# A running maximum over 512 positions, taken as four chunks of 128 on four partitions and spread by transposes

## The chip, the cores and the metric

The kernel runs on one core of a Trainium2 chip. The metric is the device time of one execution in microseconds (us): the median of several runs. The core has five engines that run side by side and wait for one another by semaphores: PE (TensorE, matrix products), DVE (VectorE), ACT (ScalarE), POOL (GpSimd) and SP (SyncE, here a queue of transfers).

## The reference

`x` is 8 rows of 512 positions of 128 numbers. Each row goes through a layer norm with a per-row scale and shift, then through a gated recurrent attention (head size 64), is added to `x`, and then goes through a second norm and a mixture of 8 experts of which each position takes 2. All of it is in 32-bit floating point. The part that the change touches is the running maximum `m_t` of the recurrence:

```
m_t = maximum(zf_t + m, zi_t)
i_p = exp(zi_t - m_t)
f_p = exp(zf_t + m - m_t)
C_t = f_p * C + i_p * (v_t k_t^T)
n_t = f_p * n + i_p * k_t
h   = o_t * (C_t q_t) / max(|n_t . q_t|, 1)
```

With F_t the running sum of `zf` and a_t = zi_t - F_t, the maximum less F_t is M_t = max(a_1 ... a_t). The whole recurrence of a row is then a masked product: the weight of position s in position t is exp(a_s - M_t) for s <= t.

## The kernel before

Every engine has its own program, written out by hand. A program is a sequence of bodies, one for each value of `b` from -2 to 7, and each body walks 16 steps `t` from 3 to 18. In one body three rows are in hand at once. Row `b` passes through the experts. Row `b+1` finishes its attention and computes its expert gates (the parts called `end`). Row `b+2` starts its attention (the parts called `start`, present for b = -2 to 5, eight bodies). In bodies 0 to 5 all three are there; these are called the full turns here. In bodies -2 and -1 there is no expert work yet, so POOL has nothing to split, and PE fills its time with products that `keep_busy` issues.

The expert work sets the pace. It has N = 16 pieces n (8 experts of 2 halves). For each, PE makes an "up" product in three parts (L1000 to L1002) into one of four banks; DVE clips and gates it into `hg` (L797); ACT rounds it into `hg_hi` (L498); the remainder `hg_lo = hg - hg_hi` is made by POOL (L446) for pieces 1 and 8 to 15 and by DVE (L809) for the others; and three steps later PE makes the "down" product in three parts (L1009, L1010, L1020). Each engine puts the attention's and the gates' operations between these pieces, in the order of the program text. Below, hg(12) means the `hg` of piece 12, and up(13) the up product of piece 13.

The stretch around the change is steps 11 to 15 of the row that starts:

- DVE makes `a_col` (L769): 128 partitions, 4 columns, one column for each chunk of 128 positions.
- PE turns it into one row of 512 on one partition by four transposes (L941), then makes the scores of chunk 0 (L877, L878).
- DVE runs a scan with max over that row (L773, `m_row`). The scan stands behind hg(12), the difference `top_d` of the two best expert logits (L684) and the four index searches (L686), and ahead of hg(13).
- PE spreads `m_row` over 128 partitions by a product of depth one with a row of ones (L952), into bank `bB`.
- DVE adds the causal mask (`mb`, L776); ACT makes the weights `ew` = exp(a_s - M_t) from it (L477, L479).

The gates of the other row are made in the same steps on DVE: `top_d`, the index searches, then, behind hg(13), `top_s`, `gate_a`, `gate_b`, `top_g` (L731, L734), two products and the sum `gates` (L739), and after that `mb`. On ACT the exponential `top_e` of `top_d` (L529) stands in step 12, between `hg_hi` of piece 11 and of piece 12, since an engine takes its instructions in order:

```
if live(t - 1):
    act.wait_ge(s_hg, b * N + t)
    a.activation(hg_hi[k][:, :], hg[k][:, :], ACT.Copy)
if t == 12 and end:
    act.wait_ge(s_td, m1 + 1)
    a.activation(top_e2[:, :], top_d[:, :], ACT.Exp)
```

In step 14 PE transposes the gates into bank 3 (L1027). ACT then makes the first `ew` (which waits for `mb`) and after it copies the gates out (`gate_rows` L541, `gateT` L542). Bank 3 is also the bank of every fourth up product, so up(15) waits for `gateT`.

Of the kernel before, what the change touches and what calls it, by code (L numbers as in the profile page):

```python
# [5 lines left out]
def adaln_mlstm_moe_kernel(  # L6
# [42 lines left out]
    ALU = mybir.AluOpType  # L49
    ACT = mybir.ActivationFunctionType  # L50

    P = 128
    B, T, D = x_in.shape
# [3 lines left out]
    NT = T // P  # L57
# [8 lines left out]
    NVO = NZ + DH  # L66
# [15 lines left out]
    with ctx:  # L82
        def sb(name, shape, dt=fp32):
            return ctx.enter_context(nc.sbuf_tensor(name, shape, dt))

        def sem(name):
            return ctx.enter_context(nc.semaphore(name))


        ident = sb("ident", [P, P])  # L90
# [3 lines left out]
        mean_col = sb("mean_col", [P, 1])  # L94
        neg_row = sb("neg_row", [1, T])
        iota_e = sb("iota_e", [P, E])
# [64 lines left out]
        a_col = sb("a_col", [P, NT])  # L161
        m_row = sb("m_row", [1, T])
        mb = sb("mb", [P, NT, P])
# [88 lines left out]
        s_a = sem("s_a")  # L252
        s_aT = sem("s_aT")
        s_M = sem("s_M")
        s_Mb = sem("s_Mb")
# [130 lines left out]
        def _(pool):  # L386
# [13 lines left out]
            g.memset(mean_col[:, :], 1.0 / D).then_inc(s_const, 1)  # L400
            g.memset(neg_row[:, :], -3e38).then_inc(s_const, 1)
            for e in range(E):
# [152 lines left out]
        def _(dve):  # L555
# [12 lines left out]


            v.memset(gateT[:, :].bitcast(fp32), 0.0).then_inc(s_zero, 1)  # L570

# [92 lines left out]
            def body(b, end, start, ahead, live, first=False):  # L664
                m1, m2 = b + 1, b + 2

                def middle(t):

                    if end:
# [6 lines left out]
                        if t == 11:  # L676

                            dve.wait_ge(s_lgp, m1 + 1)
                            v.tensor_tensor(lg[:, :, :], bC[:, 0:NT * E].rearrange("p (j e) -> p j e", j=NT),
                                            br_bc[:, :].unsqueeze(1).to_broadcast([P, NT, E]), ALU.add).then_inc(s_lg, 1)  # L680
                        if t == 12:

                            dve.wait_ge(s_mx, m1 + 1)
                            v.tensor_tensor(top_d[:, :], mx[:, :, 1], mx[:, :, 0], ALU.subtract).then_inc(s_td, 1)  # L684
                            for j in range(NT):
                                last = v.max_index(ix[:, j, :], mx[:, j, :], lg[:, j, :])  # L686
                            last.then_inc(s_ix, 1)
# [24 lines left out]
                def after(t):  # L712
# [27 lines left out]
                    if start:  # L740
# [29 lines left out]
                        if t == 12:  # L770

                            dve.wait_ge(s_aT, m2 + 1)
                            v.tensor_tensor_scan(m_row[0:1, :], bA[0:1, :], neg_row[0:1, :], -3e38, ALU.max, ALU.max).then_inc(s_M, 1)  # L773
                        if t == 13:
# [61 lines left out]

            F0 = 8
            pv = bA[:, 0:NT * NS].rearrange("p (j n) -> p j n", j=NT)
# [12 lines left out]
        def _(pe):  # L851
# [28 lines left out]
            def chain(b, end, start, t):  # L880
# [47 lines left out]
                if start:  # L928
# [9 lines left out]
                    if t == 12:  # L938
                        pe.wait_ge(s_a, m2 + 1)
                        for j in range(NT):  # L940
                            last = t_.transpose(bA[0:1, j * P:(j + 1) * P], a_col[:, j:j + 1], ident[:, :])  # L941
                        last.then_inc(s_aT, 1)
                        if end:

                            pe.wait_ge(s_lg, m1 + 1)
                        pe.wait_ge(s_qz, m2 + 1)
                        scores(0, bC[:, 0:T])
                    if t == 13:

                        pe.wait_ge(s_zo, m2 + 1)  # L950
                        pe.wait_ge(s_M, m2 + 1)
                        t_.matmul(bB[:, :], ones[0:1, :], m_row[0:1, :], start=True, stop=True).then_inc(s_Mb, 1)  # L952
                    if t == 14:
# [105 lines left out]

            F0 = 8  # L1060
            body(-2, False, True, True, lambda n: False, first=True)
# [32 lines left out]
```

## Time and profile before

| What | Value |
|---|---|
| time, median of 3 runs | 358.75 us (358.61 to 359.09) |
| time of the profiled execution | 354.73 us |
| its span, first to last instruction | 353.0 us |
| busy: PE, DVE, ACT, POOL | 320.5, 279.6, 158.6, 170.1 us |
| chain that ended last, by engine | PE 43%, DVE 37%, POOL 5%, DMA 4%, ACT 4% |
| mean granted clock of PE | 0.984 of full speed |

The busy time of an engine is the time in which it has an instruction in hand; matrix products overlap, so a busy PE need not be at its peak. The chain is the sequence of work that ended last, followed back from the last instruction, at each step to what released it or to the instruction before it on its engine. A timeline row gives the start of an instruction, its duration, engine, line, operation, output and inputs with their shapes, and in brackets the engine's idle time before it and what ended that.

### The profile page before, as it was taken

What the parts mean: (1) busy time and instruction counts of PE and PEld (TensorE: products, weight loads), DVE (VectorE), ACT (ScalarE), POOL (GpSimd) and SP (SyncE); (2) the same over time, 40 slices, a digit from 0 to 9 for tenths busy, and PEclk for the clock granted to TensorE, in tenths of its full rate; (3) what the DMA queues carried; (4) which work ended last, traced back from release to release, by engine and by line L of the source; (5) the groups of instructions that cost most, each with busy time, mean ns of one, the idle gap of its engine ahead of it and who ended that gap; (6) DMA issues with size and microseconds to landing.
All of it is one profiled execution on the core that took longest, in us unless ns stands there. A gap on an engine that the chain in (4) does not pass through costs nothing.

```text
span 353.0 us, 4976 instructions
## 1 busy us (share of the span) xinstructions
PE 320.5 (91%) x1712; PEld 257.9 (73%) x1712; DVE 279.6 (79%) x799; ACT 158.6 (45%) x292; POOL 170.1 (48%) x177
## 2 busy tenths in 40 slices
PE   2999978799899998999899989998999989887995
PEld 2887865678587867887687858785888668665883
DVE  5576783699869996899699987999679967775774
ACT  1432423254454636545546554544545354244442
POOL 7610640158544772387417852485406821583340
PEclk9999996899999999999999999999999999999999
DMA  4850001500061005200160007000610053004301
GB/s 127 266 155 0 2 0 42 200 2 0 2 238 32 3 0 183 88 0 1 63 208 2 0 8 254 10 0 0 229 45 0 0 154 117 1 1 124 147 0 30
DMA packets 13710, 24.13 MB, mean 68 GB/s; under 512 B 1771, under 2 KB 8086, under 8 KB 12662
## 3 DMA queue, kind: packets, MB, share of 16 engines
q1 hardware_dynamic: 13458, 23.69, 20.7%
q8 instruction: 13, 0.21, 0.2%
q14 instruction: 11, 0.09, 0.1%
q10 hardware_dynamic: 164, 0.07, 0.1%
q0 software_dynamic: 64, 0.07, 0.1%
HBM read 21.59 MB, written 2.23 MB: 67 GB/s over the span
## 4 chain that ended last, share of the span: by engine, by line
PE 43%; DVE 37%; POOL 5%; DMA 4%; ACT 4%; issue 4%; SPq 1%; DVEq 0%; POOLq 0%
DVE hg L797 10%; PE bank L1000 5%; PE bank L1002 5%; PE bank L967 5%; PE bank L1001 5%; PE bank L1010 4%; PE bank L1009 4%; PE bank L1020 4%; DVE hg_lo L809 2%; PE bank L900 2%; DVE stats L560 2%; DVE m_row L773 2%; DMA gate_bc<-gates_d 2%; DVE zp L759 2%; DVE zo L748 2%
## 5 line engine op out<-in xcount | busy, mean ns | idle before, releaser
L446 POOL TENSOR_TENSOR hg_lo<-hg,hg_hi 128x512 fp32r<-128x512 f32 x69 | 88.1, 1286 | 81.2 <-ACT hg_hi L498 81.2
L797 DVE SCALAR_TENSOR_TENSOR hg<-bank,neg_b,gate_bc 128x512 f32<-128x512 f32 x128 | 94.6, 743 | 35.9 <-PE bank L1002 24.0
L498 ACT ACTIVATE hg_hi<-hg 128x512 fp32r<-128x512 f32 x128 | 79.7, 628 | 90.6 <-DVE hg L797 89.2
L1000 PE MATMUL bank<-h_hi,w_hi 128*128 128x512 f32 x128 | 58.4, 456 | 9.7 <-ACT gateT L542 9.7
L1010 PE MATMUL bank<-hg_hi,w_lo 128*128 128x512 f32 x128 | 51.1, 399 | 0.0
L1001 PE MATMUL bank<-h_hi,w_lo 128*128 128x512 f32 x128 | 50.9, 397 | 0.0
L1002 PE MATMUL bank<-h_lo,w_hi 128*128 128x512 f32 x128 | 50.8, 397 | 0.0
L1009 PE MATMUL bank<-hg_hi,w_hi 128*128 128x512 f32 x128 | 50.6, 395 | 0.0
L1020 PE MATMUL bank<-hg_lo,w_hi 128*128 128x512 f32 x128 | 50.5, 394 | 0.0
L415 POOL TENSOR_SCALAR var_eps<-mv 128x4 f32<-128x4 f32 x16 | 4.9, 305 | 80.4 <-DVE mv L566 80.4
L809 DVE TENSOR_TENSOR hg_lo<-hg,hg_hi 128x512 fp32r<-128x512 f32 x59 | 42.3, 718 | 0.5
L1000 PEld LDWEIGHTS bank<-h_hi,w_hi 128*128 128x128 f32 x128 | 24.4, 191 | 20.2 <-issue 10.7
L1002 PEld LDWEIGHTS bank<-h_lo,w_hi 128*128 128x128 f32 x128 | 24.3, 190 | 5.8
L1010 PEld LDWEIGHTS bank<-hg_hi,w_lo 128*128 128x128 f32 x128 | 24.2, 189 | 5.8
L1009 PEld LDWEIGHTS bank<-hg_hi,w_hi 128*128 128x128 f32 x128 | 24.2, 189 | 5.7
L1020 PEld LDWEIGHTS bank<-hg_lo,w_hi 128*128 128x128 f32 x128 | 24.2, 189 | 5.6
L1001 PEld LDWEIGHTS bank<-h_hi,w_lo 128*128 128x128 f32 x128 | 24.5, 191 | 4.0 <-issue 1.4
L477 ACT ACTIVATE ew<-mb,a_col 128x128 f32<-128x128 f32 x32 | 11.7, 391 | 24.9 <-DVE mb L776 24.9
L967 PEld LDWEIGHTS bank<-vs,ew 128*128 128x128 f32 x160 | 19.4, 196 | 4.1 <-DVE ew L662 3.7
L967 PE MATMUL bank<-vs,ew 128*128 128x65 f32 x160 | 19.5, 278 | 3.1 <-DVE ew L662 3.1
L974 PEld LDWEIGHTS bank<-ones,ident 128*128 128x128 f32 x108 | 16.1, 216 | 5.3 <-issue 5.1
L422 POOL TENSOR_TENSOR rstd<-var_eps,minus_half 128x4 f32<-128x4 f32 x16 | 19.3, 1204 | 0.0
(163 smaller groups left out, 552.4 us busy)
## 6 DMA issues: line engine op xcount, KB each, us to landing
gate_bc<-gates_d SPq DMA_DIRECT2D x8, 1024.0 KB, 7.1
gate_bc<-gates_d SPq DMA_DIRECT2D x16, 256.0 KB, 3.7
gate_bc<-gates_d SPq DMA_DIRECT2D x8, 512.0 KB, 4.9
out_dram<-x_all SPq DMA_DIRECT2D x8, 256.0 KB, 2.3
w_raw<-in_L_ffn_W_dram SPq DMA_DIRECT2D x1, 1024.0 KB, 8.6
x_all<-in_L_attn_x_dram SPq DMA_DIRECT2D x2, 256.0 KB, 3.8
wmod_sb<-in_L_wmod_dram SPq DMA_DIRECT2D x1, 384.0 KB, 4.4
gates_d<-gate_rows SPq DMA_DIRECT2D x8, 16.0 KB
```

The source lines that it names most:

```text
L422: g.tensor_tensor(rstd[k][:, :], var_eps[k][:, :], minus_half[:, :], ALU.pow).then_inc(s_rs[k], 1)
L446: g.tensor_tensor(hg_lo[k][:, :], hg[k][:, :], hg_hi[k][:, :].bitcast(fp32), ALU.subtract).then_inc(s_lo_pool, 1)
L498: a.activation(hg_hi[k][:, :], hg[k][:, :], ACT.Copy).then_inc(s_hghi, 1)
L797: v.scalar_tensor_tensor(hg[k][:, :], up_bank[n % 4][:, :], neg_b1[:, n:n + 1], gate_bc[own % 2][:, n // NU, :], ALU.max, ALU.mult).then_i ...
L809: v.tensor_tensor(hg_lo[k][:, :], hg[k][:, :], hg_hi[k][:, :].bitcast(fp32), ALU.subtract).then_inc(s_lo_dve, 1)
L967: last = t_.matmul(bA[:, q * NS:(q + 1) * NS], ew[:, o:o + P], vs[:, j, :], start=j == 0, stop=j == q)
L1000: t_.matmul(dst, w_hi, hx, start=True, stop=False)
L1001: t_.matmul(dst, w_lo, hx, start=False, stop=False)
L1002: t_.matmul(dst, w_hi, hl, start=False, stop=True).then_inc(s_up, 1)
L1009: t_.matmul(y_bank[:, :], w_hi, hg_hi[k][:, :], start=n == 0, stop=False)
L1010: t_.matmul(y_bank[:, :], w_lo, hg_hi[k][:, :], start=False, stop=False)
L1020: t_.matmul(y_bank[:, :], w_hi, hg_lo[k][:, :], start=False, stop=n == N - 1).then_inc(s_dn, 1)
```

## The change

The transposed `a_col` is left as four rows of 128 on four partitions (one transpose in place of four), at a free place in bank `bA`. DVE scans the four chunks side by side (`m_chunk`). PE transposes the result back into columns, twice: each position's own value, and each chunk's last value repeated over all partitions. A second scan of three elements makes the maximum over the chunks before (`m_before`, whose first column is set to -3e38 once), and one operation takes the larger of the two (`m_col`). PE then spreads each column of `m_col` by a transpose of a broadcast 128x128 operand, four in all, in place of the product of depth one. The scan of the chunks moves ahead of `top_d` on DVE; PE waits for it behind the scores of chunk 0.

```diff
-        neg_row = sb("neg_row", [1, T])
+        neg = sb("neg", [P, P])
...
-        m_row = sb("m_row", [1, T])
+        m_chunk = sb("m_chunk", [NT, P])
+        m_before = sb("m_before", [P, NT])
+        m_col = sb("m_col", [P, NT])
...
-            g.memset(neg_row[:, :], -3e38).then_inc(s_const, 1)
+            g.memset(neg[:, :], -3e38).then_inc(s_const, 1)
...
+            v.memset(m_before[:, 0:1], -3e38).then_inc(s_Mz, 1)
...
+                    if t == 12 and start:
+
+                        dve.wait_ge(s_aT, m2 + 1)
+                        v.tensor_tensor_scan(m_chunk[:, :], bA[0:NT, M0:M0 + P], neg[0:NT, :], -3e38, ALU.max, ALU.max).then_inc(s_Mc, 1)
+                    if end:
                         if t == 12:
 
                             dve.wait_ge(s_mx, m1 + 1)
...
-                            dve.wait_ge(s_aT, m2 + 1)
-                            v.tensor_tensor_scan(m_row[0:1, :], bA[0:1, :], neg_row[0:1, :], -3e38, ALU.max, ALU.max).then_inc(s_M, 1)
+                            dve.wait_ge(s_McT, m2 + 1)
+                            v.tensor_tensor_scan(m_before[:, 1:NT], bA[:, M1 + NT:M1 + 2 * NT - 1], neg[:, 0:NT - 1], -3e38,
+                                                 ALU.max, ALU.max).then_inc(s_Mp, 1)
+                            dve.wait_ge(s_Mp, m2 + 1)
+                            v.tensor_tensor(m_col[:, :], bA[:, M1:M1 + NT], m_before[:, :], ALU.max).then_inc(s_M, 1)
...
-                        for j in range(NT):
-                            last = t_.transpose(bA[0:1, j * P:(j + 1) * P], a_col[:, j:j + 1], ident[:, :])
-                        last.then_inc(s_aT, 1)
+                        t_.transpose(bA[0:NT, M0:M0 + P], a_col[:, :], ident[:, :]).then_inc(s_aT, 1)
                         if end:
 
                             pe.wait_ge(s_lg, m1 + 1)
                         pe.wait_ge(s_qz, m2 + 1)
                         scores(0, bC[:, 0:T])
+
+                        pe.wait_ge(s_Mc, m2 + 1)
+                        t_.transpose(bA[:, M1:M1 + NT], m_chunk[:, :], ident[0:NT, 0:NT])
+                        t_.transpose(bA[:, M1 + NT:M1 + 2 * NT], m_chunk[:, P - 1:P].to_broadcast([NT, P]),
+                                     ident[0:NT, 0:NT]).then_inc(s_McT, 1)
...
-                        t_.matmul(bB[:, :], ones[0:1, :], m_row[0:1, :], start=True, stop=True).then_inc(s_Mb, 1)
+                        for j in range(NT):
+                            last = t_.transpose(bB[:, j * P:(j + 1) * P], m_col[:, j:j + 1].to_broadcast([P, P]), ident[:, :])
+                        last.then_inc(s_Mb, 1)
...
-            F0 = 8
+            F0, M0 = 8, 2 * NVO + 8
+            M1 = M0 + P
```

On DVE, step 12 of a full turn, from hg(12) to `top_s`. Before (a scan is listed under the name SCALAR_TENSOR_TENSOR; the brackets name the semaphores that an instruction waits for):

```order
L797 SCALAR_TENSOR_TENSOR hg<-bank,neg_b,gate_bc 128x512 [waits s_up]
L684 TENSOR_TENSOR top_d<-mx 128x4 [waits s_mx]
L686 MAX_INDEX ix<-mx,lg 128x8 x4
L773 SCALAR_TENSOR_TENSOR m_row<-bank,neg_row 1x512 [waits s_aT]
L797 SCALAR_TENSOR_TENSOR hg<-bank,neg_b,gate_bc 128x512 [waits s_up]
L691 TENSOR_SCALAR top_s<-top_e 128x4 [waits s_te]
```

The same place after the change:

```order
L812 SCALAR_TENSOR_TENSOR hg<-bank,neg_b,gate_bc 128x512 [waits s_up]
L691 SCALAR_TENSOR_TENSOR m_chunk<-bank,neg 4x128 [waits s_aT]
L696 TENSOR_TENSOR top_d<-mx 128x4 [waits s_mx]
L698 MAX_INDEX ix<-mx,lg 128x8 x4
L785 SCALAR_TENSOR_TENSOR m_before<-bank,neg 128x3 [waits s_McT]
L788 TENSOR_TENSOR m_col<-bank,m_before 128x4 [waits s_Mp]
L812 SCALAR_TENSOR_TENSOR hg<-bank,neg_b,gate_bc 128x512 [waits s_up]
L703 TENSOR_SCALAR top_s<-top_e 128x4 [waits s_te]
```

The scan that stood behind `top_d` and the index searches stands ahead of them, shorter, and two small operations take its old place ahead of hg(13).

On PE, steps 12 and 13 of a full turn, from the transposes of `a_col` to the spread of the maximum. Before:

```order
L941 MATMUL bank<-ident,a_col 1x128 [waits s_a]
L941 MATMUL bank<-ident,a_col 1x128 x3
L877 MATMUL bank<-qq,kk 128x512 [waits s_qz,s_lg]
L878 MATMUL bank<-qz,kk 128x512
L1000 MATMUL bank<-h_hi,w_hi 128x512 [waits s_hg]
L1001 MATMUL bank<-h_hi,w_lo 128x512
L1002 MATMUL bank<-h_lo,w_hi 128x512
L1009 MATMUL bank<-hg_hi,w_hi 128x512 [waits s_hghi]
L1010 MATMUL bank<-hg_hi,w_lo 128x512
L1020 MATMUL bank<-hg_lo,w_hi 128x512 [waits s_lo_pool]
L952 MATMUL bank<-m_row,ones 128x512 [waits s_M,s_zo]
```

The same place after the change:

```order
L956 MATMUL bank<-ident,a_col 4x128 [waits s_a]
L893 MATMUL bank<-qq,kk 128x512 [waits s_qz,s_lg]
L894 MATMUL bank<-qz,kk 128x512
L964 MATMUL bank<-ident,m_chunk 128x4 [waits s_Mc]
L965 MATMUL bank<-ident,m_chunk 128x4
L1021 MATMUL bank<-h_hi,w_hi 128x512 [waits s_hg]
L1022 MATMUL bank<-h_hi,w_lo 128x512
L1023 MATMUL bank<-h_lo,w_hi 128x512
L1030 MATMUL bank<-hg_hi,w_hi 128x512 [waits s_hghi]
L1031 MATMUL bank<-hg_hi,w_lo 128x512
L1041 MATMUL bank<-hg_lo,w_hi 128x512 [waits s_lo_pool]
L972 MATMUL bank<-ident,m_col 128x128 [waits s_M,s_zo]
```

Three transposes go; two small ones, with a wait for the scan, now stand between the scores and up(13); and four transposes stand where the product of depth one stood.

## Rows read from the trace of the kernel before

**Rows 1.** The page, the chain that ended last, by engine.
```profile
PE 43%; DVE 37%; POOL 5%; DMA 4%; ACT 4%; issue 4%; SPq 1%; DVEq 0%; POOLq 0%
```
**Rows 2.** The chain in order of time (start, us, what): row 0, then a full turn.
```profile
27.70 1.06 PE bank L952 x2
...
209.02 0.49 ACT gateT L542
...
222.44 0.44 PE bank L910 x4
```
**Rows 3.** Timeline of DVE in the same full turn, steps 12 and 13 (start, us).
```profile
201.72 0.75 DVE L797 SCALAR_TENSOR_TENSOR hg<-bank,neg_b,gate_bc 128x512 f32<-128x512 f32 x1
202.38 0.26 DVE L684 TENSOR_TENSOR top_d<-mx 128x4 f32<-128x4 f32 x1
...
203.12 1.19 DVE L773 TENSOR_TENSOR_SCAN m_row<-bank,neg_row 1x512 f32<-1x512 f32 x1
204.25 0.71 DVE L797 SCALAR_TENSOR_TENSOR hg<-bank,neg_b,gate_bc 128x512 f32<-128x512 f32 x1
204.89 0.24 DVE L691 TENSOR_SCALAR top_s<-top_e 128x4 f32<-128x4 f32 x1
...
205.44 0.16 DVE L734 TENSOR_TENSOR top_g<-top_g,top_e 128x4 f32<-128x4 f32 x1
...
205.87 1.17 DVE L739 TENSOR_TENSOR gates<-gate_a,gate_b 128x32 f32<-128x32 f32 x1
206.97 0.68 DVE L776 TENSOR_TENSOR mb<-bank,far 128x512 f32<-128x512 f32 x1
```
**Rows 4.** Timeline of POOL in the same stretch.
```profile
201.33 1.29 POOL L446 TENSOR_TENSOR hg_lo<-hg,hg_hi 128x512 fp32r<-128x512 f32 x1 [0.59 <-ACT hg_hi L498]
202.57 1.29 POOL L446 TENSOR_TENSOR hg_lo<-hg,hg_hi 128x512 fp32r<-128x512 f32 x1
203.82 1.28 POOL L446 TENSOR_TENSOR hg_lo<-hg,hg_hi 128x512 fp32r<-128x512 f32 x1
205.70 1.29 POOL L446 TENSOR_TENSOR hg_lo<-hg,hg_hi 128x512 fp32r<-128x512 f32 x1 [0.60 <-ACT hg_hi L498]
```
**Rows 5.** Timeline of ACT in the same stretch.
```profile
202.68 0.21 ACT L529 ACTIVATE top_e<-top_d 128x4 f32<-128x4 f32 x1 [0.77 <-DVE top_d L684]
202.79 0.62 ACT L498 ACTIVATE hg_hi<-hg 128x512 fp32r<-128x512 f32 x1
204.99 0.63 ACT L498 ACTIVATE hg_hi<-hg 128x512 fp32r<-128x512 f32 x1 [1.59 <-DVE hg L797]
```
**Rows 6.** Timeline of PE in the same turn: up(13), first and last part; up(15), first.
```profile
202.85 0.39 PE L1000 MATMUL bank<-h_hi,w_hi 128*128 128x512 f32 x1
...
203.31 0.39 PE L1002 MATMUL bank<-h_lo,w_hi 128*128 128x512 f32 x1
...
209.64 0.47 PE L1000 MATMUL bank<-h_hi,w_hi 128*128 128x512 f32 x1 [1.42 <-ACT gateT L542]
```
**Rows 7.** Timeline of body 6, the gates' steps on DVE and POOL beside them.
```profile
314.87 0.15 DVE L691 TENSOR_SCALAR top_s<-top_e 128x4 f32<-128x4 f32 x1
314.94 0.18 DVE L693 TENSOR_TENSOR gate_a<-iota_e,ix 128x32 f32<-128x32 f32 x1
315.04 1.28 DVE L694 TENSOR_TENSOR gate_b<-iota_e,ix 128x32 f32<-128x32 f32 x1
...
314.94 1.33 POOL L446 TENSOR_TENSOR hg_lo<-hg,hg_hi 128x512 fp32r<-128x512 f32 x1
```
**Rows 8.** Body -1: the chain's spread of the maximum, DVE's timeline, a window with PEclk.
```profile
52.84 2.04 PE bank L952 x2
...
50.77 0.17 DVE L684 TENSOR_TENSOR top_d<-mx 128x4 f32<-128x4 f32 x1
...
52.00:53.00 1.00, 0.94 (x5) 0.68 (x5) 1.00 (x5) 0.00 (x0) 0.00 (x0) 0.50 0.00 0
```
**Rows 9.** The scan of three elements, by line: ns minimum, median, maximum.
```profile
L759 DVE TENSOR_TENSOR_SCAN zp<-ones,zg x8: 164/892/931, 20.8 to 273.9; 128x3 f32<-128x3 f32 x8
```

More of the change, by code:

```diff
@@ L253, in adaln_mlstm_moe_kernel @@
         s_aT = sem("s_aT")
+        s_Mc = sem("s_Mc")
+        s_McT = sem("s_McT")
+        s_Mz = sem("s_Mz")
+        s_Mp = sem("s_Mp")
         s_M = sem("s_M")
@@ L1058, in body @@
                     last.then_inc(s_yT, 1)
-            F0 = 8
+            F0, M0 = 8, 2 * NVO + 8
+            M1 = M0 + P
             body(-2, False, True, True, lambda n: False, first=True)
```

## The prediction, made before the changed kernel ran

> **What bounds the kernel now.** I read the chain that ended last first. It lies on PE for 43% and on DVE for 37% [rows 1], so it changes sides: for most of a full turn PE works without a stop, and for some 15 us DVE leads. The change sits where DVE leads, and the way back to PE is in the chain and the timelines: `mb` starts on DVE at 206.97 [rows 3], ACT makes the first weights and then `gateT` at 209.02 [rows 2], and PE, which has been idle for 1.42 us, starts up(15) at 209.64 [rows 6]. From `mb` to up(15) is 2.67 us of steps in a row. A full turn therefore gets longer or shorter by what `mb` moves.
>
> Next I asked why `mb` starts as late as 206.97. The timeline of DVE has no idle time there, but some of its operations are far too long. `gates`, 32 elements, takes 1.17 us [rows 3], while `gate_a` of the same size takes 0.18 [rows 7]. `gates` starts at 205.87, when POOL has been in an `hg_lo` since 205.70, and it ends at 207.04, 0.05 after POOL's 206.99 [rows 3, 4]. `top_s` (204.89 to 205.13) ends 0.03 after POOL's 205.10, `top_d` (202.38 to 202.64) 0.02 after POOL's 202.62; with POOL idle in body -1 the same `top_d` takes 0.17 in place of 0.26 [rows 3, 4, 8]. So these operations, whose inputs all lie in SBUF, stand still until the running instruction of POOL is over. Operations with one input in PSUM (`hg`, `m_row`, `mb`) do not, nor do the index searches. Body 6 shows the order: `gate_a` started at 314.94 with POOL's next instruction and got through in 0.18; `gate_b`, 0.10 later, stood for 1.28 [rows 7]. Whoever asks first, goes first.
>
> The Trainium skill, "SBUF — State Buffer", section "Who interferes with whom", has this as a rule: a VectorE instruction with two SBUF inputs contends with a GpSimd instruction that reads SBUF, the first to issue holds the shared port for its whole length, and one with at most one SBUF input, outside the two-port modes, does not contend. The trace agrees (1.17 and 1.28 us against 0.18). By the rule the sum below holds; if the long rows were chance, it would be that of the second rival.
>
> **The change in a full turn.** Times are those of the turn in the rows; the six full turns have the same phases.
>
> *The scan.* It goes ahead of `top_d`. 512 elements took 1.19 [rows 3], three took 0.164 at least [rows 9]; a line through both gives 0.42 for 128, and the two are its bounds. hg(12) ends at 202.47, its follower starts 0.09 earlier, so the scan runs from 202.38 to 202.80. The transpose that it waits for stands where the four stood and is ready before that.
>
> *top_d, the costly step.* Before, it asked at 202.38 and slipped in when POOL's instruction ended at 202.62. Behind the scan it asks at about 202.72. POOL has then been in its next instruction since 202.57, until 203.86 [rows 4]. So `top_d` ends at 203.88, not 202.64: **1.24 us late**. This hardly hangs on the scan's price: anything over 0.2 us misses the gap.
>
> *DVE behind it.* The searches end 0.56 after `top_d` (202.64 to 203.20 before, 0.08 after the start of `m_row` behind them): 204.44. `m_before` and `m_col` read PSUM and should not stand. I take 0.16 [rows 9] and 0.17 (`top_d` with POOL idle, same size), less 0.08 of overlap with what runs ahead, and 0.03 for the wait between them: 204.71. Their bounds are 0.2, and 1.3 if each waited for POOL. hg(13) then ends 0.65 later, as it did behind the scan: 205.36, where it was 204.96.
>
> *ACT and POOL.* On ACT `top_e` waits for `top_d`, and `hg_hi` of piece 12 is queued behind it. That one starts 0.15 after `top_d`'s end and takes 0.62 [rows 5]: 204.03 to 204.65. POOL, which had worked without a pause, waits for it, starts at 204.73 instead of 203.82, and is done at 206.01. Its next instruction can start 0.74 after hg(13)'s end (204.96 to 205.70 before): 206.10.
>
> *The gates.* `top_s` asks at 205.29, in the middle of POOL's instruction, and ends at 206.04, 0.03 after it; before, 205.13. `gate_a` follows at once. `gate_b` asks 0.02 after `top_s`'s end (315.04 against 315.02, rows 7), at 206.06, which is 0.04 ahead of POOL's 206.10: I take it that it passes. `top_g` asks 0.31 after `top_s`'s end, at 206.35, finds POOL busy and stands until 207.39 plus 0.02. From its end to the start of `gates` is 0.27: 207.68. POOL has nothing more to do, so `gates` takes 0.18 and `mb` starts 0.07 before its end: **207.79 in place of 206.97, 0.82 us late**.
>
> *PE.* It waits for the scan behind the scores and issues two small transposes, so up(13) moves from 202.85 [rows 6] to about 203.2: the scan's end at 202.80, two transposes of 0.11 (a quarter of the 0.44 for four, rows 2), and the handover. It is done 0.85 after its start (202.85 to 203.70), at 204.05; hg(13) now wants it only at 204.6. The late `top_d` covers it; without that cover hg(13) would wait for it, as in the second rival. The spread of the maximum is done on PE long before 207.8, so what it saves is worth nothing here. Six full turns: 6 x 0.82 = **+4.9 us**.
>
> **Bodies -2 and -1.** POOL is idle there in these steps, nothing stands, and the spread of the maximum is in the chain. In body -1 it takes 2.04 us [rows 8], at a granted clock of 0.50, half of 2.4 GHz. Four transposes take 0.44 [rows 2] at the full clock, so 0.88 here: 1.16 less. PE's wait for the scan and the two transposes give 0.2 back: -1.0. In body -2 it takes 1.06 [rows 2] against 0.44, with 0.2 given back: -0.4. Together **-1.4**, between 0 (if something else is late there) and -1.8. The larger constant and the memset are made while the first inputs are still loading: nothing.
>
> **Sum.** +4.9 - 1.4 = +3.5. The profiled execution took 354.73, 1.1% under the median of 358.75 of the other runs; the phases inside a turn should not differ, so I add the sum to the median: **362.3 us, 1.0% slower**. A measurement of this kernel can tell 0.2% from no change, 0.7 us.
>
> **Rivals.**
>
> *One more blocked step.* `gate_b` has only 0.04 us over POOL. If it loses, it stands until 207.44; the rest of the small steps (0.74 from `top_s` to `gates` before, less the 0.20 of `gate_a` and `gate_b`) puts `gates` at 207.98 and `mb` at 208.09: 1.12 a turn, 6.7 in six, 358.75 + 6.7 - 1.4 = 364.1. For it: the margin is within the error of the two new small operations, and 0.05 off them decides.
>
> *Faster: top_d is not caught.* The point is whether `top_d` asks before POOL's 202.57, that is whether the scan takes under 0.2 us; its lower bound is 0.164. Then hg(13) is held by up(13) at 204.1 and ends 0.15 earlier than before; but `top_s` still stands until 205.13, POOL starts its last instruction that much earlier, and `gate_b`'s or `gates`' wait for it ends at about the old time. The full turns gain nothing, and bodies -2 and -1 leave 357.4, 0.4% faster. Against it: the scan's time grows with its length, 1.19 against 0.164.
>
> *A smaller delay.* If POOL's pause lets `top_s` and the gates' steps through, only the 0.40 of hg(13) is left: 6 x 0.40 - 1.4 = +1.0, 359.8. Against it: `top_s` would have to ask before 204.73.
>
> *The scan is not shorter.* At 1.19 it ends at 203.57, and `top_d` still ends at 203.88: the same time as forecast.
>
> **How the numbers follow.** Forecast 0.45; one more blocked step 0.27; a smaller delay 0.08; these three are slower, with 0.03 for something worse (a lower clock in PE's longer wait): 0.83. `top_d` not caught, or no standing at all: 0.12 faster. Gains and losses that cancel: 0.05. The range of 8 in 10 leaves out the faster and the unchanged cases and the worst one: from 359.5, just under the smaller delay, to 365.2, which is the blocked step with a third of the early gain missing, and a little more.
>
> **What would show it.** Right: `top_d` lasts about 1.2 us and ends 0.02 after POOL; `top_e`'s idle time grows by as much; a pause of 0.9 in POOL before the third `hg_lo`; `top_g`, not `gates`, lasts over 1 us; up(15) starts after 2.2 us of idle time, not 1.42; `m_before` and `m_col` are short. Wrong: `top_d` at 0.26 or less, `m_before` as long as POOL's instruction, or the same idle time ahead of up(15).

## The result, and the profile after

The changed kernel takes **363.6 us** (median of 4 runs, 362.5 to 364.0) where the kernel before, on the same chip, takes 358.9 (4 runs, 358.6 to 359.1). The comparison gives a ratio of 1.0173 with an interval of [1.0129, 1.0216]; the two medians alone give 1.013, the lower end of it. It is slower, as forecast. The time lies in the range (359.5 to 365.2), and the loss, 4.7 us by the medians, is larger than the 3.5 of the sum.

From the page of the changed kernel: the busy line, and PE's granted clock in 40 slices of 9 us (tenths of full speed, 9 for 90% or more).

```profile
PE 320.8 (89%) x1720; PEld 263.1 (73%) x1720; DVE 283.4 (78%) x816; ACT 158.6 (44%) x292; POOL 169.9 (47%) x177
...
PEclk9999968699999999999899999999999989998998
```

The clock line of the kernel before:

```profile
PEclk9999996899999999999999999999999999999999
```

Busy times have hardly moved: PE 320.5 to 320.8, DVE 279.6 to 283.4. The span has grown by 9.0 us (353.0 to 362.0). The pair of profiles exaggerates the loss, since the profiled run of before had a mean granted clock of 0.984 and that of after 0.964, and the clock of one and the same kernel changes from run to run (below). So I read the difference by stages first.

**Where the 9.0 us are.** Two instructions of ACT cut the program at the same places in both kernels: the first `h_hi` of a row, with which its expert work begins, and `gateT`, which up(15) waits for. In the full turn of [rows 3 to 6], timeline of ACT, kernel before:

```profile
197.31 0.77 ACT L487 ACTIVATE h_hi<-bank,mods 128x512 fp32r<-128x512 f32 x1
...
208.93 0.57 ACT L542 ACTIVATE gateT<-bank 8x512 fp32r<-8x512 f32 x1
```

The same in the changed kernel, with the two instructions that stand queued between:

```profile
201.32 0.77 ACT L493 ACTIVATE h_hi<-bank,mods 128x512 fp32r<-128x512 f32 x1
...
207.92 0.21 ACT L535 ACTIVATE top_e<-top_d 128x4 f32<-128x4 f32 x1 [1.99 <-DVE top_d L696]
208.03 0.62 ACT L504 ACTIVATE hg_hi<-hg 128x512 fp32r<-128x512 f32 x1
...
213.73 0.57 ACT L548 ACTIVATE gateT<-bank 8x512 fp32r<-8x512 f32 x1
```

From one to the other is 11.62 us before (208.93 - 197.31) and 12.41 after. Every difference of this kind, from start to start:

| Stage | before | after | difference |
|---|---|---|---|
| start of the program to `h_hi` of body -1 | 46.43 | 46.29 | -0.1 |
| body -1, `h_hi` to `gateT` | 10.98 | 10.20 | -0.8 |
| `gateT` of body -1 to `h_hi` of body 0 | 26.98 | 28.33 | +1.4 |
| `h_hi` to `gateT`, six full turns | 11.61 to 11.62 | 12.40 to 12.42 | +4.8 |
| `gateT` to the next `h_hi`, four of six | 26.02 to 26.03 | 25.90 to 25.91 | -0.5 |
| the same, the other two | 26.02, 24.82 | 27.47, 26.28 | +2.9 |
| body 6 and the rest | 10.13 + 33.85 | 10.41 + 34.90 | +1.3 |

The sum is +9.0. The +4.8 is the change's own work. The four positive differences of over 1 us are another thing: in each of them PE ran for about 3 us longer at half its clock than before. A window of the changed kernel in one of the two long passes from `gateT` to `h_hi` (length, busy us of PE, PEld, DVE, ACT, POOL, then PEclk, DMA share and GB/s):

```profile
176.00:180.00 4.00, 4.00 (x15) 3.20 (x14) 3.08 (x6) 2.10 (x5) 1.59 (x2) 0.68 0.71 193
```

The kernel before has 1.00 throughout these two passes.

**The steps of a turn.** Timeline of DVE of the changed kernel, to be laid beside [rows 3]:

```profile
206.40 0.40 DVE L691 TENSOR_TENSOR_SCAN m_chunk<-bank,neg 4x128 f32<-4x128 f32 x1
206.73 1.16 DVE L696 TENSOR_TENSOR top_d<-mx 128x4 f32<-128x4 f32 x1
...
208.37 0.13 DVE L785 TENSOR_TENSOR_SCAN m_before<-bank,neg 128x3 f32<-128x3 f32 x1
208.53 0.16 DVE L788 TENSOR_TENSOR m_col<-bank,m_before 128x4 f32<-128x4 f32 x1
...
209.27 0.77 DVE L703 TENSOR_SCALAR top_s<-top_e 128x4 f32<-128x4 f32 x1
...
210.05 0.18 DVE L706 TENSOR_TENSOR gate_b<-iota_e,ix 128x32 f32<-128x32 f32 x1
210.15 0.17 DVE L743 RECIPROCAL top_g<-top_s 128x4 f32<-128x4 f32 x1
210.36 1.04 DVE L746 TENSOR_TENSOR top_g<-top_g,top_e 128x4 f32<-128x4 f32 x1
...
211.65 0.19 DVE L751 TENSOR_TENSOR gates<-gate_a,gate_b 128x32 f32<-128x32 f32 x1
211.76 0.68 DVE L791 TENSOR_TENSOR mb<-bank,far 128x512 f32<-128x512 f32 x1
```

POOL in the same stretch, beside [rows 4]:

```profile
205.35 1.29 POOL L452 TENSOR_TENSOR hg_lo<-hg,hg_hi 128x512 fp32r<-128x512 f32 x1 [0.59 <-ACT hg_hi L504]
206.60 1.27 POOL L452 TENSOR_TENSOR hg_lo<-hg,hg_hi 128x512 fp32r<-128x512 f32 x1
208.73 1.28 POOL L452 TENSOR_TENSOR hg_lo<-hg,hg_hi 128x512 fp32r<-128x512 f32 x1 [0.86 <-ACT hg_hi L504]
210.10 1.27 POOL L452 TENSOR_TENSOR hg_lo<-hg,hg_hi 128x512 fp32r<-128x512 f32 x1
```

`top_d` now asks at 206.73, behind the scan. POOL's instruction ended at 206.64 and the next had started at 206.60, so `top_d` stands until 207.89, 0.02 after POOL's 207.87. ACT's `top_e` waits for it (1.99 us idle), `hg_hi` is queued behind `top_e`, and POOL pauses for 0.86 until that `hg_hi` is done. `top_s` then falls into the middle of POOL's third instruction (0.77 in place of 0.24), `gate_b` gets ahead of the fourth by 0.05, `top_g` stands for 1.04, and `gates` is short again because POOL has no more to do.

The timeline of PE shows where this arrives, beside [rows 6]:

```profile
211.90 0.60 PE L1048 MATMUL bank<-ident,gates 128*8 128x128 f32 x4 [1.05 <-DVE gates L751]
...
214.44 0.47 PE L1021 MATMUL bank<-h_hi,w_hi 128*128 128x512 f32 x1 [1.43 <-ACT gateT L548]
```

PE idles 1.05 us before the gates' transposes and 1.43 before up(15), 2.48 together, where it idled for 1.42 before.

### The profile page after: what moved, and what is told of

It reads as the page before. It is cut to its first block, busy times and chain, and to the rows that moved or that the text cites. A ratio compares the mean times of both kernels' runs of the same rounds, so it can differ in the third digit from the quotient of the medians.

```text
span 362.0 us, 5009 instructions
## 1 busy us (share of the span) xinstructions
PE 320.8 (89%) x1720; PEld 263.1 (73%) x1720; DVE 283.4 (78%) x816; ACT 158.6 (44%) x292; POOL 169.9 (47%) x177
## 4 chain that ended last, share of the span: by engine, by line
PE 47%; DVE 38%; ACT 5%; POOL 4%; issue 3%; DMA 3%; SPq 1%; DVEq 0%; POOLq 0%
DVE hg L812 9%; PE bank L1021 6%; PE bank L1023 5%; PE bank L988 5%; PE bank L1022 5%; PE bank L1041 5%; PE bank L1030 5%; PE bank L1031 4%; DVE hg_lo L824 2%; PE bank L916 2%; DVE top_d L696 2%; DVE top_g L746 2%; DVE stats L566 2%; DVE zo L760 2%; DVE zp L771 2%
## 5 line engine op out<-in xcount | busy, mean ns | idle before, releaser
L1021 PE MATMUL bank<-h_hi,w_hi 128*128 128x512 f32 x128 | 59.2, 463 | 9.8 <-ACT gateT L548 9.8
L1023 PE MATMUL bank<-h_lo,w_hi 128*128 128x512 f32 x128 | 51.7, 404 | 0.0
L1041 PE MATMUL bank<-hg_lo,w_hi 128*128 128x512 f32 x128 | 51.7, 404 | 0.0
L1030 PE MATMUL bank<-hg_hi,w_hi 128*128 128x512 f32 x128 | 51.4, 401 | 0.0
L988 PEld LDWEIGHTS bank<-vs,ew 128*128 128x128 f32 x160 | 20.9, 209 | 4.8 <-DVE ew L669 4.2
L988 PE MATMUL bank<-vs,ew 128*128 128x65 f32 x160 | 21.0, 291 | 3.7 <-DVE ew L669 3.7
L995 PE MATMUL bank<-ones,ident 128*128 128x128 f32 x108 | 19.1, 317 | 0.5 <-DVE b_lo L654 0.5
```

The costliest lines, as they stand in the source:

```text
L988: last = t_.matmul(bA[:, q * NS:(q + 1) * NS], ew[:, o:o + P], vs[:, j, :], start=j == 0, stop=j == q)
L1021: t_.matmul(dst, w_hi, hx, start=True, stop=False)
L1023: t_.matmul(dst, w_hi, hl, start=False, stop=True).then_inc(s_up, 1)
L1030: t_.matmul(y_bank[:, :], w_hi, hg_hi[k][:, :], start=n == 0, stop=False)
L1041: t_.matmul(y_bank[:, :], w_hi, hg_lo[k][:, :], start=False, stop=n == N - 1).then_inc(s_dn, 1)
```

## The experiments

The theory: DVE's small operations stand while POOL is in an instruction; the change loses 0.8 us a turn because its first scan moves `top_d` out of a gap between two of them; and half-clock stretches of PE account for the rest of the 9.0 us between the two profiles. The rivals: the new operations (two scans, `m_col`, the extra handover from PE) cost the time by themselves; or PE's additional transposes do. The measure for the first part is the stretch from `h_hi` to `gateT` in a full turn, since the half-clock stretches that the full turns lost time in all lie outside it: 11.62 before, 12.41 after. Kernels measured together share the runs of the kernel before on their chip.

**1. `top_d` ahead of the scan (after, one operation moved).**

```diff
+                    if end and t == 12:
+                        dve.wait_ge(s_mx, m1 + 1)
+                        v.tensor_tensor(top_d[:, :], mx[:, :, 1], mx[:, :, 0], ALU.subtract).then_inc(s_td, 1)
                     if t == 12 and start:
 
                         dve.wait_ge(s_aT, m2 + 1)
...
-
-                            dve.wait_ge(s_mx, m1 + 1)
-                            v.tensor_tensor(top_d[:, :], mx[:, :, 1], mx[:, :, 0], ALU.subtract).then_inc(s_td, 1)
```

> The changed kernel with one edit on DVE: top_d stands ahead of the scan of the chunks, as it stood ahead of the row's scan before. Theory (top_d misses the gap between two of POOL's instructions, and ACT, POOL and the gates follow): top_d lasts 0.26 us again, POOL works without a pause through its three hg_lo, gates stands until POOL's last one is over as in the kernel before, and the stretch from h_hi to gateT in a full turn is 11.5 to 11.7 us, where it is 11.61 in the kernel before and 12.41 in the changed one. Time 357.5 to 359.5. Rival (the two small operations on DVE and PE's wait for the scan cost the time): the stretch stays at 12.1 us or more, time 361 to 363.

Measured: 357.55 us (356.71 to 358.86, 10 runs) against 357.80, ratio 1.0004 [0.9968, 1.0040]. The stretch is 11.65. Timeline of DVE:

```profile
202.64 0.27 DVE L690 TENSOR_TENSOR top_d<-mx 128x4 f32<-128x4 f32 x1
202.83 0.40 DVE L694 TENSOR_TENSOR_SCAN m_chunk<-bank,neg 4x128 f32<-4x128 f32 x1
...
203.70 0.13 DVE L785 TENSOR_TENSOR_SCAN m_before<-bank,neg 128x3 f32<-128x3 f32 x1
203.86 0.16 DVE L788 TENSOR_TENSOR m_col<-bank,m_before 128x4 f32<-128x4 f32 x1
204.50 0.75 DVE L812 SCALAR_TENSOR_TENSOR hg<-bank,neg_b,gate_bc 128x512 f32<-128x512 f32 x1 [0.47 <-PE bank L1023]
...
206.14 1.17 DVE L751 TENSOR_TENSOR gates<-gate_a,gate_b 128x32 f32<-128x32 f32 x1
```

All the new operations are there, and the loss is not. `top_d` is in its gap again, and `gates` stands for 1.17 as in [rows 3]. The rivals fall as the cause of the loss: what costs time is the order. Two more things show. POOL is in an instruction from 202.83 to 204.13 here, and `m_before` and `m_col`, with one input in PSUM, take 0.13 and 0.16 beside it; in the changed kernel POOL had been idle at that moment, so its trace could not show that they don't stand. And hg(13) now waits for PE (0.47): the shorter scans do make DVE earlier, but up(13) comes later. From the timeline of PE, the wait for `m_chunk` and up(13):

```profile
203.29 0.22 PE L964 MATMUL bank<-ident,m_chunk 4*128 4x4 f32 x1 [0.37 <-DVE m_chunk L694]
...
203.50 0.50 PE L1021 MATMUL bank<-h_hi,w_hi 128*128 128x512 f32 x1
```

up(13) starts 1.52 us after hg(12), which starts at 201.98 here; in the kernel before it was 1.13 [rows 3, 6]. The new handover takes back what the shorter scan gives, so nothing is won.

The Trainium skill, "SBUF — State Buffer", section "Who interferes with whom", says that a VectorE instruction with at most one SBUF input, outside the two-port modes, does not contend with GpSimd. The 0.13 and 0.16 agree with it.

**2. The old scan in the new place (before, its scan of 512 moved ahead of `top_d`).**

```diff
+                    if t == 12 and start:
+
+                        dve.wait_ge(s_aT, m2 + 1)
+                        v.tensor_tensor_scan(m_row[0:1, :], bA[0:1, :], neg_row[0:1, :], -3e38, ALU.max, ALU.max).then_inc(s_M, 1)
+                    if end:
                         if t == 12:
...
-                        if t == 12:
-
-                            dve.wait_ge(s_aT, m2 + 1)
-                            v.tensor_tensor_scan(m_row[0:1, :], bA[0:1, :], neg_row[0:1, :], -3e38, ALU.max, ALU.max).then_inc(s_M, 1)
```

> The kernel before with one edit on DVE: the scan of the row of 512, unchanged, moved ahead of top_d. Theory (order): the scan ends at about 203.57 on the scale of the rows, top_d stands until 203.88 all the same, hg_hi of piece 12 is late behind top_e, and gate_a or gate_b stands behind POOL once more; the stretch from h_hi to gateT is 12.5 to 12.8 us against 11.61, time 363.5 to 366. Rival (what costs is in the new operations, not the order): time within 0.5 us of the kernel before, 358.4 to 359.4.

Measured: 367.29 us (365.62 to 368.95, 4 runs), ratio 1.0285 [1.0234, 1.0336]; the stretch is 12.61. Timeline of DVE, then of POOL:

```profile
170.68 1.21 DVE L684 TENSOR_TENSOR_SCAN m_row<-bank,neg_row 1x512 f32<-1x512 f32 x1
171.82 0.16 DVE L689 TENSOR_TENSOR top_d<-mx 128x4 f32<-128x4 f32 x1
...
173.11 1.00 DVE L696 TENSOR_SCALAR top_s<-top_e 128x4 f32<-128x4 f32 x1
...
174.13 1.27 DVE L699 TENSOR_TENSOR gate_b<-iota_e,ix 128x32 f32<-128x32 f32 x1
```

```profile
172.82 2.53 POOL L446 TENSOR_TENSOR hg_lo<-hg,hg_hi 128x512 fp32r<-128x512 f32 x2 [0.86 <-ACT hg_hi L498]
```

The order alone, with none of the new operations, costs 1.0 us a turn, more than the change. `top_d` ends 1.4 us after hg(12) whether it stands behind POOL or behind a long scan, and POOL pauses for the same 0.86. Here `gate_b` loses to POOL's next instruction and stands for 1.27: the forecast's first rival, seen in another kernel. The time is above the range expected of it by 1.3 us; in its profile three of the five passes from `gateT` to `h_hi` between full turns last 27.4 to 27.6 us instead of 26.03, and that of body -1 lasts 30.27 instead of 26.98, each with the clock at half for a while.

**3. ACT's `top_e` one step later (after).** `top_d` still stands; only the `hg_hi` behind `top_e` is set free.

```diff
-                    if t == 12 and end:
+                    if t == 13 and end:
 
                         act.wait_ge(s_td, m1 + 1)
                         a.activation(top_e2[:, :], top_d[:, :], ACT.Exp).then_inc(s_te, 1)
```

> The changed kernel with one edit on ACT: top_e stands behind hg_hi of piece 12, not ahead of it, so that hg_hi and with it POOL's hg_lo no longer wait for top_d. Theory: top_d still lasts 1.16 us, but POOL works without a pause, top_s is free, and only gates stands at the end; of the 0.80 us that a full turn lost up to gateT half comes back: 11.9 to 12.1 us, time 360.5 to 362. Rival (the late hg(13) on DVE carries the whole delay, ACT's order is harmless): 12.3 us or more, time 363 or more.

Measured: 357.97 us (357.27 to 361.62, 10 runs), ratio 1.0027 [0.9988, 1.0065]; the stretch is 12.01. Timeline of DVE, then of POOL:

```profile
203.97 1.17 DVE L696 TENSOR_TENSOR top_d<-mx 128x4 f32<-128x4 f32 x1
...
206.53 0.16 DVE L703 TENSOR_SCALAR top_s<-top_e 128x4 f32<-128x4 f32 x1
```

```profile
202.59 3.78 POOL L452 TENSOR_TENSOR hg_lo<-hg,hg_hi 128x512 fp32r<-128x512 f32 x3 [0.59 <-ACT hg_hi L504]
```

POOL's pause is gone, `top_s` finds it idle (206.53 is after 206.37) and takes 0.16, and half of the 0.8 is back. So the chain through ACT and POOL is real, and it makes half of the loss; the other 0.4 is DVE's own lateness. The time came out 2.5 us below what was expected; its profile has no half-clock stretch in the full turns, which the expectation had not counted on.

**4. PE kept busy in its new wait (after).** Four idle products, whose result nobody reads, stand ahead of PE's wait for `gates`.

```diff
                     if t == N - 2 and end:
 
-                        pe.wait_ge(s_gates, b + 2)
                         if live(N - 5):
                             pe.wait_ge(s_hg, b * N + (N - 4))
+                            keep_busy(4)
+                        pe.wait_ge(s_gates, b + 2)
```

> The changed kernel with four idle products of 128 columns on PE in the full turns while it waits for the gates, into a bank whose reader is done (their result is never read). The stretch from h_hi to gateT should stay at 12.41 us. Theory that PE's longer wait is why its granted clock falls to half for some 3 us in one or two turns of the changed kernel: fewer such stretches, mean clock 0.98 or more, time 361 to 362.5. Rival (the falls of the clock have another cause): mean clock 0.964 to 0.970 as in the changed kernel, time 362.5 to 364.

Measured: 359.91 us (359.01 to 361.13, 4 runs), ratio 1.0105 [1.0055, 1.0155]; the stretch is 12.43, unchanged. The clock line of its page:

```profile
PEclk9999988799999999999999999999999999998999
```

In the view of PE's waits the one before the transposes is down from 8.5 us in total to 2.0. In this profile the two low slices in the full turns are gone, and every pass from `gateT` to `h_hi` between full turns takes 25.9. The mean granted clock of its four runs is 0.976 to 0.981, of the changed kernel's four 0.964 to 0.970. By the times, the two intervals of the ratio overlap, so the gain is likely and not shown. The mean clocks point the same way and settle no more: experiment 1 has 0.966 to 0.971 without a low stretch in a full turn of its profile, and the kernel before goes from 0.963 to 0.985 on one chip. The time is 1.1 us below what was expected, and the clock in part below the 0.98. What is left of the loss is 1.05%, with the same stretch in every full turn.

**5. `mb` ahead of `gates` (the kernel of experiment 1, and DVE's order changed once more).**

```diff
+                        if start and live(0):
+                            dve.wait_ge(s_Mb, m2 + 1)
+                            v.tensor_tensor(mb[:, :, :], bB[:, :].rearrange("p (j t) -> p j t", j=NT),
+                                            far[:, :].unsqueeze(1).to_broadcast([P, NT, P]), ALU.add).then_inc(s_mask, 1)
...
-                        if t == 13:
+                        if t == 13 and not (end and live(0)):
```

> The changed kernel with top_d ahead of the scan (as in e1) and, in the full turns, mb ahead of gates on DVE: gates stands until POOL's hg_lo is over in any case, so mb, which reads PSUM, should fit into that time. Theory (gates stands until a fixed moment that POOL sets): gates ends where it ended in e1, mb costs nothing ahead of it, ACT's first weights are done before the gates arrive, and the stretch from h_hi to gateT falls from 11.65 us to 10.8 to 11.1. Time 352.5 to 355. Rival (gates is long by itself, or DVE is the limit): mb only moves gates by its own 0.6 us, the stretch stays at 11.5 us or more, time 356.5 to 358.5.

Measured: 352.07 us (351.81 to 354.82, 4 runs) against 357.39, ratio 0.9877 [0.9779, 0.9974]; the stretch is 10.94. Timeline of DVE:

```profile
204.60 0.68 DVE L752 TENSOR_TENSOR mb<-bank,far 128x512 f32<-128x512 f32 x1
205.20 0.71 DVE L755 TENSOR_TENSOR gates<-gate_a,gate_b 128x32 f32<-128x32 f32 x1
```

`mb`, which reads PSUM, works while POOL's instruction runs, and `gates` stands only for the rest of it. Hiding `mb` in that time is worth 0.7 us a turn; what it is worth if `gates` doesn't stand at all, the next three show. The time is 0.4 us below what was expected.

**6 to 8. Piece 13 taken from POOL,** so that DVE makes `hg_lo(13)` itself, in three kernels: that of experiment 1 (6), before (7) and after (8).

```diff
-    POOL_STEPS = (1, 8, 9, 10, 11, 12, 13, 14, 15)
+    POOL_STEPS = (1, 8, 9, 10, 11, 12, 14, 15)
```

> The changed kernel with top_d ahead of the scan (as in e1), and hg_lo of piece 13 made by DVE, not by POOL, so that POOL is idle when gates asks. Theory (standing behind POOL): gates lasts 0.19 us where it lasted 1.17, mb starts about 1.0 us earlier, and the stretch from h_hi to gateT is 10.6 to 10.8 us. Time 351 to 353.5. Rival (DVE is the limit in this stretch, and 0.7 us more work on it makes it longer): 11.6 us or more, time 357.5 or more.

> The kernel before with the one edit that hg_lo of piece 13 is made by DVE, not by POOL. It tells whether the new running maximum is worth anything once gates no longer stands behind POOL. Theory: gates is free here too, but PE, which still makes the product of depth one, reaches the gates' transposes some 0.15 us later than in e6: the stretch from h_hi to gateT is 10.75 to 10.95 us against 11.61, time 352 to 354.5, that is 0 to 1.5 us behind e6. Rival (the scan of 512 on DVE is then what sets the end, and the change is worth its 0.4 to 0.8 us on DVE): 11.1 us or more, time at least 2.5 us behind e6.

> The changed kernel, scan ahead of top_d as it was, with hg_lo of piece 13 made by DVE. Theory: top_d still stands for 1.16 us and top_s for 0.77 behind the late hg_lo of piece 12, but top_g no longer stands: of the delay at gateT 0.9 us goes, the stretch is 11.4 to 11.7 us, time 356 to 358.5, 5 us behind e6. Rival (the second standing, of top_g, is the whole loss and the first is harmless): the stretch is as short as in e6, 10.6 to 10.8 us.

| Kernel | us, runs | ratio to before | stretch |
|---|---|---|---|
| 6, `top_d` first, no piece 13 on POOL | 347.00 (346.61 to 348.01, 4) | 0.9719 [0.9634, 0.9804] | 10.65 |
| 7, before, no piece 13 on POOL | 352.01 (351.50 to 353.10, 4) | 0.9849 [0.9765, 0.9933] | 10.80 |
| 8, after, no piece 13 on POOL | 355.12 (353.54 to 356.86, 10) | 0.9950 [0.9905, 0.9995] | 11.53 |

Timeline of DVE in kernel 6:

```profile
202.61 0.19 DVE L751 TENSOR_TENSOR gates<-gate_a,gate_b 128x32 f32<-128x32 f32 x1
202.72 0.68 DVE L791 TENSOR_TENSOR mb<-bank,far 128x512 f32<-128x512 f32 x1
```

And in kernel 8:

```profile
202.28 1.16 DVE L696 TENSOR_TENSOR top_d<-mx 128x4 f32<-128x4 f32 x1
...
204.83 0.76 DVE L703 TENSOR_SCALAR top_s<-top_e 128x4 f32<-128x4 f32 x1
```

With one instruction of POOL less beside them `gates` no longer stands in 6; in 8 `top_d` and `top_s` still do. Each of the kernels is faster for it, 7 without any part of the change. Kernel 6 against 8 is the order of `top_d` and the scan again, with a free end: 0.88 us a turn in the stretch, which is 5.3 in six turns, and 8 us in the time. Of the rest the profiles show 1.4 after the last `gateT` (33.5 in 6, 34.9 in 8), where 8 has a low stretch of the clock; the time of 8 is 0.9 us below what was expected. Kernel 6 is 4 us under what was expected, which had counted the full turns alone: against experiment 1 body 6 gains 0.9 too (10.14 to 9.23, `h_hi` to `gateT`) and the rest of the program 2.3 (35.84 to 33.52), where experiment 1 has a low stretch of the clock. Kernel 6 against 7 is not settled. The stretch differs by 0.15, as expected, and the pass behind it by 0.11, which makes 1.6 us in six turns; the times differ by 5.0, where 0 to 1.5 was expected. In the profile of 7 PE waited 1.99 us for `vs` at 22.46 (0.54 in the kernel before), its granted clock was 0.62 from 24 to 28 us, and `h_hi` of body -1 came at 49.11 where 6 had it at 46.03. Up to there kernel 7 runs the same instructions as the kernel before, which had it at 46.43, so these 3 us are not the price of the old maximum. Another 1.7 lie after the last `gateT` (35.2 against 33.5), with the clock at half for 3 us in 7. How much of this is in the medians, one profile of each can't show.

**9 and 10. PE kept busy in body -1's wait.** Ten idle products, whose result nobody reads, ahead of the wait for `ew`, in after (10) and in the kernel of experiment 6 (9).

```diff
+                    if opening and t == N + 2:
+                        pe.wait_ge(s_ghi, b + 2)
+                        keep_busy(10)
                     chain(b, end, start, t)
```

> The changed kernel with ten idle products of 128 columns on PE in body -1, in the wait ahead of the 20 products of weights and values (3.73 us in the changed kernel, 3.07 in the kernel before), into a bank whose readers are done (their result is never read). Theory (the gain of the early bodies is given back because PE, ready earlier, waits longer there and then runs the products at half clock): the 20 products take 2.2 to 3.0 us, where they took 4.53, and the stretch from gateT of body -1 to the h_hi of body 0 falls from 28.33 us to 26.0 to 27.2. Time 1 to 2.5 us less than the changed kernel. Rival (the clock there does not hang on that wait, or something else sets the end of the stretch): 28.0 us or more.

> The kernel of e6 (top_d ahead of the scan, hg_lo of piece 13 on DVE) with the same ten idle products. Theory: the same 1 to 2.5 us less than e6, 344.5 to 346, the best version so far. Rival: no difference from e6, 346.5 to 348.

Kernel 10: 361.18 us (359.56 to 361.94, 4 runs) against 355.75, ratio 1.0118 [1.0024, 1.0211]. From `gateT` of body -1 to `h_hi` of body 0 it takes 25.17, below the 26.0 expected at least, where after took 28.33 and before 26.98. The profiles of experiments 1, 3 to 6 and 8, which have the new maximum, show 28.19 to 28.48 there, so the 28.33 is no chance of one run. The 20 products with `ew` are in the chain of all three; kernel before, after, and 10 in this order (start, us):

```profile
63.69 3.01 PE bank L967 x20
```

```profile
62.59 4.53 PE bank L988 x20
```

```profile
63.33 2.45 PE bank L988 x20
```

PE's idle time before them is in its timelines, in the same order:

```profile
63.69 0.55 PE L967 MATMUL bank<-vs,ew 128*128 128x65 f32 x3 [3.07 <-DVE ew L662]
```

```profile
62.59 0.69 PE L988 MATMUL bank<-vs,ew 128*128 128x65 f32 x2 [3.73 <-DVE ew L669]
```

```profile
63.33 0.44 PE L988 MATMUL bank<-vs,ew 128*128 128x65 f32 x2 [1.27 <-DVE ew L669]
```

And the window from 64 to 68 us, columns as above, again before, after and 10:

```profile
64.00:68.00 4.00, 4.00 (x24) 3.71 (x23) 2.12 (x6) 1.26 (x2) 1.27 (x1) 0.68 0.57 239
```

```profile
64.00:68.00 4.00, 4.00 (x18) 3.81 (x18) 1.01 (x4) 0.63 (x1) 1.21 (x1) 0.50 0.35 145
```

```profile
64.00:68.00 4.00, 4.00 (x27) 3.58 (x27) 3.19 (x9) 1.86 (x3) 1.27 (x1) 1.00 0.52 218
```

Here the early gain went. PE is done with what stands ahead of this wait 1.8 us sooner (62.59 - 3.73 = 58.86 against 60.62), but the last part of `ew` comes only 1.1 us sooner: on DVE it is queued behind the first `hg`, which waits for a transfer, at 61.25 in after and at 62.36 before:

```profile
61.25 0.75 DVE L812 SCALAR_TENSOR_TENSOR hg<-bank,neg_b,gate_bc 128x512 f32<-128x512 f32 x1 [2.90 <-DMA gate_bc<-gates_d]
```

So PE idles longer (3.73 for 3.07), is at half its clock when the products start, and takes 1.5 us more for them. With the idle time filled, the clock stays at 1.00 and the loss is gone. The whole time of kernel 10 gains less than that shows, since a stretch of 27.47 in one full turn and a slow last turn stay, as in after.

Kernel 9: 344.68 us (343.56 to 346.47, 4 runs), ratio 0.9687 [0.9597, 0.9776], better than both kernels. From `gateT` to `h_hi` of body 0 it is 25.14, and the clock line has one low slice left:

```profile
PEclk9999998999999999999999999999999999999999
```

## Why the prediction was right, and where it was not

Each step of the full turn held, but for the place of PE's wait (below). The scan took 0.40 (0.42 forecast). `top_d` missed the gap and ended 0.02 after POOL, as written. `m_before` and `m_col` did not stand (0.13 and 0.16 for 0.16 and 0.17). POOL paused for 0.86 (0.9 forecast). `top_s` stood until POOL's end, `gate_b` got past by 0.05 (0.04 forecast), `top_g` stood in place of `gates`, and `gates` took 0.19. The result was 0.80 us a turn for 0.82, +4.8 us for +4.9. Experiments 1 to 3 show the causes: the order of `top_d` and the scan makes all of it, the queue on ACT half of it.

One reading was too wide: that operations "whose inputs all lie in SBUF" stand. The reciprocal that makes the first `top_g` has its one input in SBUF, starts 0.05 us after POOL's fourth instruction (210.15 against 210.10) and takes 0.17; it does so in all six full turns. The forecast let only the second `top_g` stand, which is what happened, so its sum is not touched.

Of the rivals, "one more blocked step" did not happen here, with 0.05 us to spare, and did in experiment 2. "`top_d` not caught" needed a scan under 0.2 us. "A smaller delay" is what experiment 3 makes of the kernel, with the same 0.40 a turn. "The scan is not shorter" had the end of `top_d` right (1.4 us after hg(12) in both), but not the same time: experiment 2 loses 1.0 us a turn with the long scan, and there `gate_b` stands in place of `top_g`, as in the first rival.

The step that was mis-sized is the early bodies, **-1.4**. Of body -2's 0.4 the profile shows 0.14 (`h_hi` of body -1 at 46.29 for 46.43). Body -1's spread of the maximum took 0.87 for the 0.88 forecast, and `gateT` of that body came 0.92 us earlier. But the sum stopped there, as if every later step would follow; the products that came next took 1.5 us more at a lower clock, and `h_hi` of body 0 came 0.4 us later than before. By this profile the term should have been +0.4. Experiment 10 shows the clock to be the cause.

The second omission is the clock in the full turns. The longer wait was to be PE's 2.2 us ahead of up(15); it came as 1.05 and 1.43, on either side of the gates' transposes, so this check was misplaced, though the sum of 2.48 was nearly right. That such waits can cost clock stood in the forecast with a chance of 0.03 only. In the profiled run two full turns lost 1.4 us each and the tail another 1.0 that way. How much of it is in a median can't be read from one profile, but the runs of the kernel before give a rough bound: on one chip its spans went from 353.0 us at a mean clock of 0.985 to 357.5 at 0.963. Beside those low ones (357.5 at 0.963, 357.6 at 0.971), the changed kernel's 362.0 at 0.964 and 360.5 at 0.970 stand 4.5 and 2.9 us higher. That the total stayed within 1.2 us of the sum owes something to luck: the early term was off by 1.8, and against it the passes from `gateT` to `h_hi` got about 0.7 shorter in six turns, which the forecast did not have (4.8 + 0.4 - 0.7 makes 4.5, beside the 4.7 of the medians). What decides in which turn a low stretch comes is open, and so are the 0.12 us that `gateT` to `h_hi` got shorter by.

## What to carry to other kernels

Before moving an instruction on DVE, look at what POOL does at both places: a small operation of the kinds that stood here (two inputs, both in SBUF, or a `tensor_scalar`) that leaves a gap between two of POOL's instructions waits for the whole next one, and what is queued behind its reader on ACT waits with it. Look for the remedy in the order (such operations into the gaps, those that read PSUM beside POOL's work, one instruction of POOL less where DVE is the bound), since here 0.5 us of DVE's work per turn was saved without any gain (one operation of 1.19 against 0.40, 0.13 and 0.16) and 0.3 us of order cost 0.8. And when a step becomes faster ahead of a wait that stays, add the longer idle time of PE to the account, with what the products behind it cost at half the clock.

## What the runs showed of the hardware

- A DVE operation that stands ends 0.02 to 0.05 us after POOL's instruction, whichever of `top_d`, `top_s`, `top_g` (the product), `gate_b`, `gates` it is. The request decides, within 0.05 us: `gate_b` at 210.05 passed POOL's 210.10, and in experiment 2 at 174.13, behind POOL's 174.05, it did not. `top_s` stands too, with a single input, in SBUF (0.77 against 0.16 with POOL idle in experiment 3), while the reciprocal, also with a single input in SBUF, took 0.17 beside POOL. The section of the Trainium skill cited above gives a reason that fits, that a `tensor_scalar` may run in a two-port mode; no run here took that mode away.
- The scan with max takes 0.13 us for 3 elements, 0.40 for 128 and 1.19 for 512 (2.1 ns for each element of a row between the last two); four rows side by side cost no more than the line through the two others gave for one.
- PE's granted clock fell from 1.00 to 0.50 (2.4 to 1.2 GHz) after waits that grew by only 0.7 to 1.1 us, in some turns and some runs; what decides in which, is open. In body -1 ten idle products in the wait kept it at 1.00 (experiments 9 and 10), which was worth 3.2 us (28.33 to 25.17), more than the whole early gain of the change; in the full turns four did so in the one profile of experiment 4.
